# A two-layer graph network kernel: hop 0 of the first graph pair as whole float32 products, its inputs loaded in halves, and a new order of the start

## The reference

```python
# layer 0, X = x, A = adj, three hops
Xw = X @ Wv + bv
sj, si = Xw @ aw[:d, 0], Xw @ aw[d:, 0]
e = leaky_relu(sj[:, None, :] + si[:, :, None] + ab[0], negative_slope=0.2)
alpha = A * exp(e)
transition = alpha / (sum(alpha, axis=-1, keepdims=True) + 1e-12)
H, Xk = 0, X
for k in range(3):
    H = H + Xk @ Wk[k] + bk[k]
    Xk = einsum('bij,bjd->bid', transition, Xk)
x = layernorm(x + relu(H))
# layer 1
x = layernorm(x + einsum('bnm,bmf->bnf', adj, x) @ w)
```

## Time and profile before

| | us |
|---|---|
| median of 3 runs (lowest, highest) | 272.84 (272.76, 273.21) |
| the profiled execution's own time | 273.95 |
| its span, first to last instruction | 272.1 |
| PE busy in the span | 266.3 |
| DVE, ACT, POOL busy | 216.8, 191.6, 190.3 |
| share of PE in the chain that ended last | 93% |

### The profile page before, as it was taken

How to read it: one execution, slowest core, us unless ns; L and a number is a source line. 1 busy time by engine, 2 the same in 40 slices (tenths; PEclk the granted TensorE clock), 3 DMA queues, 4 the chain that set the end, 5 groups by cost and what they waited for, 6 DMA issues and landing times.

```text
span 272.1 us, 6029 instructions
## 1 busy us (share of the span) xinstructions
PE 266.3 (98%) x1887; PEld 246.6 (91%) x1887; DVE 216.8 (80%) x615; ACT 191.6 (70%) x437; POOL 190.3 (70%) x412
## 2 busy tenths in 40 slices
PE   8999999999999999999999999999999999999992
PEld 3899999999999999999999999999999999999991
DVE  0677788888898888889888888988888888788994
ACT  2688677776667777666777766677766677767874
POOL 2567547788777777877778787777887777657533
PEclk9999999999999999999999999999999999999998
DMA  7858245749584378545764448844883347922214
GB/s 222 292 164 135 30 147 125 81 139 150 150 151 145 58 136 140 165 142 155 126 86 123 146 155 143 150 121 79 133 161 99 117 115 87 135 75 77 79 41 154
DMA packets 28758, 34.91 MB, mean 128 GB/s; under 512 B 7091, under 2 KB 16694, under 8 KB 28726
## 3 DMA queue, kind: packets, MB, share of 16 engines
q1 hardware_dynamic: 28016, 34.12, 56.7%
q10 hardware_dynamic: 710, 0.40, 0.5%
HBM read 26.09 MB, written 8.42 MB: 127 GB/s over the span
## 4 chain that ended last, share of the span: by engine, by line
PE 93%; DVE 2%; DMA 1%; POOL 1%; ACT 1%; issue 1%; POOLq 0%; ACTq 0%
PE ps_v L1123 30%; PE ps_y L1123 16%; PE ps_out L1123 14%; PE ps_h L1123 11%; PE ps_agg L1300 10%; PE ps_v L1233 3%; PE ps_v L1237 3%; PE ps_v L1235 3%; PE ps_agg L1123 2%; DMA WY_sb<-Wk_dram 1%; PE ps_y L1151 1%; PE ps_v L1151 1%; POOL rstd L1025 1%; DVE stats L865 0%; DVE y L878 0%
## 5 line engine op out<-in xcount | busy, mean ns | idle before, releaser
L1123 PE MATMUL ps_v<-WX_hi,XT_hi 128*128 128x512 f32 (+1 forms) x128 | 47.7, 373 | 0.0
L1123 PE MATMUL ps_v<-WX_lo,XT_hi 128*128 128x512 f32 (+1 forms) x128 | 47.4, 371 | 0.0
L1123 PE MATMUL ps_v<-WX_hi,XT_lo 128*128 128x512 f32 (+1 forms) x128 | 47.4, 371 | 0.0
L1040 POOL TENSOR_TENSOR XT_lo<-xt,XT_hi 128x512 fp32r<-128x512 f32 x32 | 41.3, 1293 | 5.4 <-DVE WX_lo L964 2.7
L1052 POOL TENSOR_TENSOR alpha<-exps,adjs 128x256 f32<-128x256 f32 x31 | 22.9, 740 | 30.3 <-ACT exps L477 30.0
L1056 POOL TENSOR_TENSOR alpha_lo<-alpha,alpha_hi 128x256 fp32r<-128x256 f32 x31 | 22.8, 734 | 18.4 <-ACT alpha_hi L486 18.4
L509 ACT ACTIVATE y<-res,offset,rstd 128x256 f32<-128x256 f32 x62 | 33.6, 590 | 0.8 <-POOL offset L1016 0.8
L1123 PE MATMUL ps_y<-WY_hi,XT_hi 128*128 128x258 f32 x112 | 34.1, 304 | 0.0
L1300 PEld LDWEIGHTS ps_agg<-adjs,y 128*128 128x128 f32 x248 | 32.0, 191 | 2.3
L1300 PE MATMUL ps_agg<-adjs,y 128*128 128x128 f32 x248 | 32.7, 275 | 0.0
L502 ACT ACTIVATE V_hi<-ps_v 128x512 fp32r<-128x512 f32 x32 | 19.1, 597 | 19.1 <-PE ps_v L1123 18.9
(11 more groups left out here) (177 smaller groups left out, 838.7 us busy)
## 6 DMA issues: line engine op xcount, KB each, us to landing
xt<-xt_dram SPq DMA_DIRECT2D x32, 256.0 KB, 5.3
nodes<-nodes_dram SPq DMA_DIRECT2D x32, 256.0 KB, 5.4
out_dram<-out_sb SPq DMA_DIRECT2D x30, 256.0 KB, 5.0
adjs<-adjs_dram SPq DMA_DIRECT2D x32, 128.0 KB, 5.3
spread<-si_rows_dram SPq DMA_DIRECT2D x29, 128.0 KB, 4.7
W_sb<-Wk_dram SPq DMA_DIRECT2D x2, 256.0 KB, 3.9
si_rows_dram<-scores SPq DMA_DIRECT2D x29, 1.0 KB, 3.6
WY_sb<-Wk_dram ACTq DMA_DIRECT2D x1, 256.0 KB, 4.1
```

Of the source, the lines that this page charges most:

```text
L1040: pool.tensor_tensor(XT_lo[k % 7][:].rearrange("p c b i -> p (c b i)"), xt_sb[k % 4][:], XT_hi[k % 7][:].rearrange("p c b i -> p (c b i)") ...
L1123: last = pe.matmul(to, a, b, start=start and n == 0, stop=stop and n == 2, skip_group_check=True)
```

## The change

For pair 0, hop 0 is now made of whole float32 products, ahead of everything else and by chunk c of the contraction (`first_hop0(c)`, four written products), and hop 2 and hop 1 are split products like those of the other pairs. X of pair 0 is loaded in two halves by SP and W0 in two halves by ACT, both by chunk; SP's wait for X of pair 0 is gone. `vectors_sb` and hop 2's W move from ACT's queue to SP's, W1 goes behind them; `w` is loaded later, X of pair 4 earlier. ACT issues a one-element exponential between W0's second half and `bk_sb`. ACT makes the high half of hop 2's W (`wy_hi`), DVE its low half, the two score columns apart. The biases are split too, and summed by two fp32r products behind `v2_lo(0)`, in `ps_y` in place of `ps_agg`. The exponentials and alphas of pair 0 stay in PSUM (`ps_out`). Pair 1's hop 2 is no longer drained in halves. `keep_warm` has five products in place of nine. On POOL the waits ahead of xt_lo(3) and of alpha(1) go, and in step 0 `norm1(0)` stands behind alpha_lo(2); on DVE `inverse(1)` stands ahead of `first_h`; on ACT alpha_hi(2) ahead of v2_hi(4). At the very end ACT takes the second standard deviation ahead of the first output of the last pair but one.

```diff
-            load_xt(0)
+            half = C * PER * P // 2
+            sp.dma_start(xt_sb[0][:, 0:half], xt[0, :, 0:half]).then_inc(first_xt_loaded, DMA)
+            sp.dma_start(xt_sb[0][:, half:2 * half], xt[0, :, half:2 * half]).then_inc(xt_loaded[0], DMA)
             sp.dma_start(WvT_sb[:], WvT.rearrange("(c p) n -> p c n", p=P)).then_inc(WvT_loaded, DMA)
+            sp.dma_start(vectors_sb[:].rearrange("p c n -> p (c n)"), vectors).then_inc(vectors_loaded, DMA)
+            load_Wk(2)
             load_Wk(1)
-            sp.wait_ge(xt_loaded[0], DMA)
-            load_Wk(0)
             load_xt(1)
+            sp.wait_ge(Wk_loaded[0], DMA)
+            load_adjs(0)
             sp.wait_ge(Wk_loaded[2], DMA)
-            load_adjs(0)
-            sp.wait_ge(Wk_loaded[1], DMA)
             load_xt(2)
...
+            act.dma_start(W0_sb[:, 0], Wk[0, 0:P]).then_inc(first_W0_loaded, DMA)
+            act.dma_start(W0_sb[:, 1], Wk[0, P:2 * P]).then_inc(Wk_loaded[0], DMA)
+            act.activation(exps[:, 0, 0:1], one, ACT.Exp)
             act.dma_start(bk_sb[:], bk).then_inc(bk_loaded, DMA)
...
+            dve.wait_ge(WY_hi_ready, 1)
+            dve.tensor_tensor(WY_lo[:, :, 0:D], WY_sb[:], WY_hi[:, :, 0:D].bitcast(F32), ALU.subtract)
             dve.wait_ge(u_done, 1)
...
+            dve.tensor_copy(WY_hi[:, :, D:D + 2], ps_u).then_inc(u_ready, 1)
+            dve.wait_ge(u_ready, 1)
+            dve.tensor_tensor(WY_lo[:, :, D:D + 2], ps_u, WY_hi[:, :, D:D + 2].bitcast(F32),
+                              ALU.subtract).then_inc(WY_ready, 1)
...
+            def first_hop0(c):
+
+                pe.wait_ge(*((first_xt_loaded, DMA) if c == 0 else (xt_loaded[0], DMA)))
+                pe.wait_ge(*((first_W0_loaded, DMA) if c == 0 else (Wk_loaded[0], DMA)))
                 X = xt_sb[0][:].rearrange("p (c b i) -> p c b i", c=C, b=PER)
+                for b in range(PER):
+                    last = pe.matmul(ps_h[:, b], X[:, c, b], W0_sb[:, c], start=b == 0 and c == 0, stop=c == C - 1,
+                                     skip_group_check=True)
+                if c == C - 1:
+                    last.then_inc(h_done, 1)
...
-            keep_warm(ps_v[:, 0], 9)
-            first_hop2(0)
+            keep_warm(ps_v[:, 0], 5)
+            first_hop0(0)
             score_weights()
-            first_hop2(1)
+            first_hop0(1)
+            score_shift()
+            hop2_and_scores(0)
             first_hop1(0)
-            score_shift()
-            first_hop1(1)
-            sum_of_biases()
             pe.wait_ge(identity_ready, 1)
             spread_scores(0)
-            hop0(0)
+            first_hop1(1)
             hop2_and_scores(1)
+            sum_of_biases()
             pe.wait_ge(ones_columns_ready, 1)
             propagate_v2(0)
```

More of the change, by code:

```diff
@@ L320, in load_xt @@
                 if k == 4:
-                    sp.wait_ge(v1_done, 1)
+                    sp.wait_ge(h_done, 1)
                 if k >= 4:
@@ L396, in step @@
                     load_adjs(k + 3)
-                if there(k + 9) and k >= -5:
+                if there(k + 9) and k >= -4:
                     load_xt(k + 9)
@@ L400, in step @@
                     load_adjs(4)
+                    sp.dma_start(w_sb[:], w.rearrange("(c p) n -> p c n", p=P)).then_inc(w_loaded, DMA)
                 if there(k - 3):
                     store(k - 3)
-            for k in range(-5, LAST + 2):
+            for k in range(-4, LAST + 2):
                 step(k)
@@ L430, in wx_hi, with bk_hi_of, wy_hi @@
             def wx_hi(n):
+                if n == 0:
+                    act.wait_ge(first_W0_loaded, DMA)
                 act.wait_ge(Wk_loaded[n], DMA)
-                act.activation(WX_hi[:, :, 1 - n], (W0_sb, W1_sb)[n][:, :, 0:D], ACT.Copy).then_inc(WX_hi_ready[n], 1)
+                act.activation(WX_hi[:, :, 1 - n], (W0_sb, W1_sb)[n][:], ACT.Copy).then_inc(WX_hi_ready[n], 1)
+            def bk_hi_of():
+                act.wait_ge(bk_loaded, DMA)
+                act.activation(bk_hi[:], bk_sb[:], ACT.Copy).then_inc(bk_hi_ready, 1)
+            def wy_hi():
+                act.wait_ge(Wk_loaded[2], DMA)
+                act.activation(WY_hi[:, :, 0:D], WY_sb[:], ACT.Copy).then_inc(WY_hi_ready, 1)
             def scores_of(k):
                 act.wait_ge(y_done, k + 1)
+                if k == 0:
+                    act.wait_ge(shift_ready, 1)
                 act.activation(scores[k % 3][:].rearrange("p n b -> p b n"), hop2(k)[:, :, D:D + 2], ACT.Identity,
                                bias=shift[:]).then_inc(scores_ready, 1)
[L439 to L449, removed]
-                last = act.activation(V2_hi[1][:, b, 0:D], hop2(1)[:, b, 0:D], ACT.Copy)
-                last.then_inc(second_v2_hi_half_ready if b == 0 else v2_hi_ready, 1)
             def v2_hi(k):
@@ L624, in _ @@
             wx_hi(0)
+            wy_hi()
+            wx_hi(1)
+            bk_hi_of()
+            xt_hi(1)
+            xt_hi(2)
+            scores_of(0)
             v2_hi(0)
-            xt_hi(1)
-            first_scores()
-            xt_hi(2)
             leaky_of(0)
@@ L643, in _ @@
             alpha_hi_of(1)
-            xt_hi(4)
             v2_hi(2)
@@ L916, in step @@
                     return
+                if k > 0 and not both_hops(k):
+                    scale_h(k)
+                inverse(k + 1)
                 if k == 0:
                     first_h()
-                elif not both_hops(k):
-                    scale_h(k)
-                inverse(k + 1)
                 if both_hops(k):
@@ L953, in split_w @@
                 dve.tensor_tensor(w_lo[:], w_sb[:], w_hi[:].bitcast(F32), ALU.subtract).then_inc(w_ready, 1)
+            bk_lo_of()
             shift_of_scores()
+            first_hop0_low()
+            first_hop1(0)
             v2_lo(0)
+            first_alpha()
+            first_hop1(1)
+            first_alpha_lo()
             bias_of_hops()
[L958 to L966 removed]
+            v2_lo(1)
             inverse(0)
             first_v()
+            first_hop0()
             v1_lo(0)
@@ L1093, in _ @@
             last.then_inc(ones_columns_ready, 1)
+            xt_lo(0)
             pool.wait_ge(vectors_loaded, DMA)
@@ L1101, in _ @@
             pool.tensor_tensor(bv_aw_sum[:], bv_aw_chunks[:, 0:1], bv_aw_chunks[:, 1:2], ALU.add).then_inc(bv_aw_ready, 1)
-            for k in range(3):
+            for k in range(1, 5):
                 xt_lo(k)
-            pool.wait_ge(WX_ready[1], 1)
-            xt_lo(3)
             alphas(1)
             alpha_lo_of(1)
-            xt_lo(4)
             xt_lo(5)
@@ L1340, in sum_of_biases @@
                 pe.wait_ge(ones_ready, 1)
-                pe.wait_ge(bk_loaded, DMA)
-                pe.matmul(ps_bias, ones[:], bk_sb[:], start=True, stop=True,
+                pe.wait_ge(bk_ready, 1)
+                pe.wait_ge(v2_lo_ready, 1)
+                pe.matmul(ps_bias, ones[:], bk_hi[:], start=True, stop=False, skip_group_check=True)
+                pe.matmul(ps_bias, ones[:], bk_lo[:], start=False, stop=True,
                           skip_group_check=True).then_inc(bias_done, 1)
```

147 lines of the change are left out of this document (55 added, 92 removed).

## The result

| | before | after |
|---|---|---|
| median of 6 runs (lowest, highest), us | 272.92 (272.76, 273.6) | 275.75 (274.73, 277.0) |
| ratio, with 95% interval | | 1.0098 (1.0083 to 1.0113) |
| the profiled execution's own time, us | 273.95 | 274.73 |
| its span, us | 272.1 | 272.9 |

The change made the kernel 1.0% slower, 2.83 us by the medians. The forecast was 270.8 us. The profiled execution of after is the fastest of its six, that of before was one of the slowest of its kernel: the two profiles lie 0.8 us apart, the medians 2.8.

The account below looks back on a forecast made before the run. TensorE was taken as the bound, busy almost throughout from 8 to 260 us, so an earlier first pair shifts everything. Gains 1.5 + 0.4 + 0.15 = 2.05 us, applied to the 272.84 median, gave 270.8 us; range 270.0 to 272.8.

Parts of the forecast that it names:

- If the level rises at 6.7 as before: Start: TensorE goes from 1.2 to 2.4 GHz during score_weights, which then end at 7.05 us.
- the level rises later: Rival: idle gaps at the start keep TensorE at 1.2 GHz longer; 272.3 us (chance 0.20) or 273.6 (0.12).
- `WvT_sb` keeps its place, and the tiny `vectors_sb` ... keeps its 5.7: Start: same 512 KB in line, so WvT_sb lands as before and vectors_sb, moved to SP, at 5.7 us.
- `WY_sb` takes the place that hop 1's W had: 6.3: Start: hop 2's W lands at 6.3 us; a rival had it a place later, 7.0, giving 271.4, chance 0.13.
- theory C: From the follow-ups: pauses and four fewer warming products make TensorE spend more of its start at 1.2 GHz.
- I apply the difference to it: Base: the profiled span's fall from 272.1 to 270.05 us, taken off the 272.84 median, gives 270.8.
- mark: First product of propagate_v2(0) on TensorE: forecast to move from 14.47 to 12.95 us, a gain of 1.5.
- `score_weights` at 5.8: Start: TensorE waits for vectors_sb until 5.8 us, then starts the eight rows of score_weights.
- Hop 2 at 8.15: Start: hop2_and_scores(0) could start at 8.15 us, with its split W ready at 8.0, no stall and no slack.
- 12 + 6 + 6 + 12 + 2 split products ... at 0.12: Hop 2 start to propagate_v2(0): 4.56 us of split products, the last two the biases, plus a 0.22 spread.
- After the mark: Stalls before 28 us for XT_lo(4) and alpha_lo(2) shrink: about 0.4 us gained, bounds 0 and 0.6.
- The tail: End: ACT's second standard deviation ahead of an output saves DVE waiting: 0.15 us, between 0 and 0.33.

Follow-up runs that it names:

- e_bwarm5: Before with five warming products in place of nine, nothing else changed: 276.57 us, ratio 1.0128.
- e_fill: After with warming products in each TensorE pause: six at the start, four behind first_hop0(0), two behind the score shift; 274.04 us, ratio 1.0040.
- e_after: The changed kernel run again unchanged, for a second profile: 276.18 us, ratio 1.0107 against before.
- e_whole: After with X0 and W0 loaded whole, vectors_sb issued by ACT, first_hop0(1) straight behind first_hop0(0), six warming products first: 275.18 us, ratio 1.0055.
- e_before: The kernel before the change run again unchanged, for a second profile: 273.02 us, ratio 0.9986.
- e_late: Before with its own start and only the late edits (alpha_hi(2), norm1(0), inverse(1), second standard deviation at the end): 272.9 us, ratio 0.9992.
- e_whole8s: Same edits to after as e_whole, but eight warming products first and bk_sb, ab_col issued behind xt_hi(0), wx_hi(0): 272.71 us, ratio 0.9975.

## Why the prediction was wrong

**Where it failed first: the level.** "If the level rises at 6.7 as before" carried the sum, and "the level rises later" had 0.32 of the chances. The prediction had both of its conditions: PE idle from 2.9 to 3.5 and from 5.2 to 5.8. `e_bwarm5` shows that fewer warming products cost before 3.4 us by themselves, and `e_fill` gives 1.9 of after's 2.8 us back. The rival had the right place, and its price of 2.8 us is near what the low level costs in `e_after`, after's usual course: 0.8 on `score_weights`, 0.9 on `first_hop0(1)`, about 1.0 on nine slow products. Its 273.6 is too low because it stands on the landings and the base below. What it did not have is the other course: the level rises early, and falls again after a pause. The Trainium skill, "TensorE: Matmul & The Clock Gate", section "Why this matters for your kernels", advises to keep TensorE continuously busy. The prediction kept that as a rival for want of a row, and the runs here bear the advice out: 3.4 us for four products fewer in `e_bwarm5`.

**Where it failed second: two landings.** "`WvT_sb` keeps its place, and the tiny `vectors_sb` ... keeps its 5.7" and "`WY_sb` takes the place that hop 1's W had: 6.3". They came at 6.4 and 7.12, in the second execution at 7.66 and 8.2. `WvT_sb`, on which `score_weights` waits as well, was hardly earlier: 6.2 and 7.4 (1.62 + 4.6, 1.61 + 5.8), where before had 5.5, so that an earlier `vectors_sb` alone could have saved 0.2 to 0.3 us. Two things were left out. Each issue on SP takes 0.4 to 0.5 us, and half an X and `vectors_sb` stand ahead of `WY_sb` now: it was issued at 2.60, the W of the earlier trace rows at 1.61. And the rate in 3 to 7 us fell from 345 GB/s to 255, and to 200 in the slower execution. With whole loads, `e_whole` has `WY_sb` at 5.8. So the halves cost about 1.1 us on `WY_sb`, one issue and a lower rate, and gained 0.8 us on a first product that then waited for `vectors_sb` anyway. What cost, by theory C, was the longer pause behind that product.

**Where it failed third: the base.** "That execution's own time was 273.95 ..., the median of the three runs is 272.84, and I apply the difference to it". The 1.1 us between the two was not noise around the span: it was the slow first rows, 2.00 us against 1.65 in `e_before`, and with them a part of the very start from which the difference was taken. The spans of before on the other chips start at 270.8, and their median is 271.4. With the 257.6 to 257.7 us that lie between mark and end in both profiles of before, a median execution has its mark near 13.75 (worked out); `e_late`, with the same start and a span of 271.4, has it at 13.88. On the chip of the prediction, where 272.84 is the median, the same sum gives 13.35. The best start measured, 13.07 in `e_whole8s`, is within 0.12 of the forecast 12.95, and its span of 270.3 within 0.25 of the forecast 270.05. Yet its median is 0.7 us below before's, not 2.05. Some 0.7 to 1.1 us of the gain (14.47 less 13.75 or 13.35) was in before's median already.

**The terms of the sum, in the profile of after.** First halves at 3.5: right (first row 3.52). `score_weights` at 5.8: 6.45. Hop 2 at 8.15: 8.82. From there to the mark 4.80: 6.75, of which 1.47 is the pace of the first fourteen starts (8.82 to 11.97, where fourteen times 0.12 is 1.68). Most of the other 0.5 is the biases: "12 + 6 + 6 + 12 + 2 split products ... at 0.12". The two short ones, from the last product of hop 2 at 14.70 to the mark, took 0.87 us with 0.17 idle, where three steps at 0.12 are 0.36; the two float32 rows that they replaced took 0.69 in before. Nothing was gained there.

**After the mark: right.** From the mark to the start of `hops(2)` are 29.47 - 15.57 = 13.90 us, before 28.90 - 14.47 = 14.43: 0.53 regained, 0.4 forecast. `e_late` has 14.14, about the half of it that belongs to alpha_lo(2). From the mark to the end of the span, however, only 0.3 is left (257.33 us, before 257.63): 0.14 of the rest is the tail, and for the last 0.1 the runs name no cause.

**The tail: wrong.** DVE's second normalisation does start 0.39 us earlier, counted from `last_stats` (1.41 us against 1.80). But its store is the third in SP's queue, and the first of the three now waits for ACT's output, which the earlier standard deviation has pushed back: SP issues it 1.46 us behind `last_stats`, before 1.42. From `last_stats` to the end of the span are 4.93 us, before 4.79; `e_late`, with the same edit, has 1.46 and 4.85. The 0.15 of the forecast is at best zero; the prediction did say that the stores are issued one after the other, and did not follow the queue.

## What to carry to other kernels

Count idle time of TensorE in the first ten microseconds as a cost twice over: the pause, and a slower pace of what comes behind it; a load that is split to start PE sooner can be a loss if it opens a pause behind the first product. Before a difference is applied to a median, see how the profiled execution stands to it and in which rows it is slower, since a part of the gain may be only that. Follow a moved load through its issuing queue as well as through the bytes ahead of it.
